# Route's shared network cut into 128 + 64 features, its list products one chunk later, the high digit's products on ScalarE

## Chip, cores, metric

The kernel runs on one NeuronCore of a Trainium2 chip. The metric is the device time of one launch in microseconds (us). Engines are named as in the profile: PE (TensorE; PEld is its weight load), DVE (VectorE), ACT (ScalarE), POOL (GpSimd), SP (SyncE, which here only issues DMAs).

## What is computed

The reference is a two-layer vision model on 8 images: patch embedding (1030 tokens of 192 features per image), retention, a mixture of experts, latent attention, a second mixture of experts. The change lies in the first mixture of experts. Its reference, cut to what matters:

```python
n = b * l                                   # 8 * 1030 tokens, d = 192
scores = sigmoid(x @ gate_weight.T)         # 16 experts
topk_score, topk_ids = top_k(scores.T, 1030)
xg = x[topk_ids]                            # each expert takes 1030 tokens
...
shared = silu(hidden_states @ Ws_g.T) * (hidden_states @ Ws_u.T) @ Ws_d.T   # 192 -> 384 -> 192
return y + shared
```

## The kernel before, in words

`phase_retention` ends with `x1T`, the normalised tokens with features on the partitions: two halves of 96 features (DP, DC = 96, 2). PE turns them (L385), ACT copies them out of PSUM (L499).

`phase_route` follows. It runs four instruction streams at once, bound only by semaphores; the order on each engine is that of the code.

- **Logits.** DVE copies the gate into a padded weight (L846), PE multiplies it with all tokens (L738), ACT applies the sigmoid.
- **The search**, LOOPS = 10 passes. Each pass finds three bits of the score threshold: DVE counts scores above a candidate (L862), PE sums the counts (`total`, L747), DVE keeps or drops the bit (L869 to L873). In between the pass does one chunk of 412 tokens of the shared network: gate and up in three slices f of 128 hidden features (`shared_up`, L715), silu on ACT (L800), the product on DVE (`shared_mult`, L825), down on PE (`shared_down`, L725), the sum with the residual on DVE (`shared_rows`, L834). SP loads and stores the rows.
- **A stretch on DVE** that turns the threshold into ranks, cut into a low digit (64 values) and a high digit (17 values), and PE turns them so that tokens lie on partitions.
- **The list stage**, NC = 10 chunks of 103 tokens, each with one more 412-token chunk of the shared network. DVE makes one-hot rows of the low digit (`hot_lo`, L928, four parts of 32 columns), of the high digit (`hit`, L933), and from `hit` two products: times the tile number (L937) and times the row number (L939), both into `hot_hi` (the trace calls it rt_wide). PE multiplies `hot_hi` with `hot_lo` (L785, 128 small products, "list products" below). `hot_lo` and `hot_hi` have two buffers each, `hit` one. POOL meanwhile issues 20 DMAs of scores (L705).

All of gate's and up's products are f32: the trace shows each as two records per product. In a chunk, slice f = 2 uses the PSUM banks of f = 0, so PE waits for the first `shared_mult`; `shared_down` waits for all three.

`phase_dispatch` and `phase_project`, late in the program, hold a shared network of the same size that is already cut into 128 + 64 (`shared_unit`, L2145 to L2151), with `pair_of` (L2132) on POOL. `phase_experts` has such a cut too. They are unchanged.

Of the kernel before, what the change touches and what calls it, by code (L numbers as in the profile page):

```python
# [16 lines left out]
B = 8  # L17
D = 192
# [220 lines left out]
def route_consts(ctx, nc):  # L239
    return buffers(ctx, nc, "rt", gate=(DP, DC, E0), same=(128, 128), before=(128, 128), consts32=(T, ROUTE_COLS), row=(T, 1),  # L240
                   wg=(DP, DC, FS0), wu=(DP, DC, FS0), wd=(128, FS0 // 128, D))


def load_route_consts(queue, inp, c, arrived):
    for dst, src in ((c["gate"][:], inp["gateT"].rearrange("(c p) e -> p c e", c=DC)),
                     (c["same"][:], inp["rt_same"]), (c["before"][:], inp["rt_before"]),
                     (c["consts32"][:], inp["rt_iota"]), (c["row"][:], inp["rt_row"]),
                     (c["wg"][:], inp["sh_gT"].rearrange("(c p) f -> p c f", c=DC)),
                     (c["wu"][:], inp["sh_uT"].rearrange("(c p) f -> p c f", c=DC)),
                     (c["wd"][:], inp["sh_dT"].rearrange("(c p) d -> p c d", c=FS0 // 128))):  # L250
        queue.dma_start(dst, src).then_inc(arrived, 16)


ROUTE_CONSTS = 16 * 8


def phase_retention(nc, psum, inp, h0, h1, xg, x1T, ident, ident_in, ret, consts_in, route, route_in):
# [5 lines left out]
    with ExitStack() as ctx:  # L263
# [105 lines left out]
        def _(pe):  # L369
# [9 lines left out]
            def turn_x1(c):  # L379

                for g in range(2):
                    pe.wait_ge(x_ready, c * 8 + (4 * g + 4))
                    for m in range(DC):
                        for b in range(HB):
                            last = pe.transpose(psum[0:DP, 2 * g + m, b * T:(b + 1) * T],  # L385
                                                x_out[:, g * HB + b, m * DP:(m + 1) * DP], ident[0:T, 0:T])
                        last.then_inc(xT_full, 1)
# [76 lines left out]
        def _(act):  # L464
# [30 lines left out]
            def x1_out(c):  # L495
                for g in range(2):
                    for m in range(DC):
                        act.wait_ge(xT_full, c * 4 + (2 * g + m + 1))
                        act.activation(x1T[:, m, g * HB:(g + 1) * HB, bass.ds(c * T, T)],  # L499
                                       bank(2 * g + m, DP, W4).rearrange("p (b t) -> p b t", b=HB),  # L500
                                       ACT.Identity).then_inc(xT_ready, 1)
# [102 lines left out]
def phase_route(nc, psum, inp, h1, xg, x1T, y, ids, ident, ident_in, consts, consts_in):  # L604
# [13 lines left out]
    with ExitStack() as ctx:  # L618
        sb, sem = names(ctx, nc)
        gate, same, before, consts32, row = (consts[n] for n in ("gate", "same", "before", "consts32", "row"))  # L620
        wg, wu, wd = (consts[n] for n in ("wg", "wu", "wd"))
        gpad = sb("rt_gpad", [DP, DC, B, 128])
        iota_lo = sb("rt_iota_lo", [T, LB], BF16)
        iota_hi = sb("rt_iota_hi", [T, HB2], BF16)
        tile0 = sb("rt_tile0", [T, 128], BF16)
# [37 lines left out]
        turned, turned_out = sem("rt_turned"), sem("rt_turned_out")  # L663
        hit_ready, hot_ready, hot_used = sem("rt_hit_ready"), sem("rt_hot_ready"), sem("rt_hot_used")
# [6 lines left out]
        h_loaded, y_stored = sem("sh_h_loaded"), sem("sh_y_stored")  # L671
# [24 lines left out]
        def _(pool):  # L696
            pool.memset(gpad[:], 0.0).then_inc(zeroed, 1)
            pool.memset(ones, 1.0).then_inc(zeroed, 1)
            pool.memset(zero[:], 0.0).then_inc(zeroed, 1)

            pool.wait_ge(turned_out, 9)
# [7 lines left out]
        def shared_up(pe, j, slices=range(FC)):  # L709

            for f in slices:
# [19 lines left out]
        def _(pe):  # L731
# [3 lines left out]
            for s, n in enumerate((W4, W4, SEQ - 2 * W4)):  # L735
                for b in range(B):
                    for k in range(DC):
# [38 lines left out]
            with pe.Fori(0, NC // 2) as i:  # L776
                for half in range(2):
                    c = i * 2 + half
                    shared_up(pe, c + LOOPS)
                    shared_down(pe, c + LOOPS)  # L780
                    pe.wait_ge(hot_ready, c + 1)
                    for b in range(B):
                        for e in range(E0):
                            q, g = e % 2, e // 2
                            last = pe.matmul(psum[LB * q:LB * q + 2 * HB2, 6, g * LB:(g + 1) * LB],  # L785
                                             hot_hi[:, half, b * E0 + e, :], hot_lo[:, half, b * E0 + e, :],
                                             start=False, stop=False, skip_group_check=True)
                    last.then_inc(hot_used, 1)
# [6 lines left out]
        def shared_silu(act, j):  # L795
            for f in range(FC):
# [6 lines left out]
        def _(act):  # L803
# [11 lines left out]
            with act.Fori(0, NC) as c:  # L815
                shared_silu(act, c + LOOPS)
# [22 lines left out]
        def _(dve):  # L839
# [3 lines left out]
            dve.wait_ge(zeroed, 3)  # L843
# [7 lines left out]
            dve.tensor_copy(tile0[:], consts32[:, LB + HB2:]).then_inc(consts_ready, 1)  # L851
# [69 lines left out]
            def list_chunk(c, half, first):  # L921
# [3 lines left out]
                if not first:  # L925
                    dve.wait_ge(hot_used, c - 1)
                for f in range(FC + 1):
                    dve.tensor_tensor(hot_lo[:, half, f * 32:(f + 1) * 32, :],  # L928
                                      lo_c[:, f * 32:(f + 1) * 32].unsqueeze(2).to_broadcast([T, 32, LB]),
                                      iota_lo[:].unsqueeze(1).to_broadcast([T, 32, LB]), ALU.is_equal)  # L930
                    if f < FC:
                        shared_mult(dve, c + LOOPS, (f,))
                dve.tensor_tensor(hit[:], hi_c.unsqueeze(2).to_broadcast([T, 128, HB2]),  # L933
                                  iota_hi[:].unsqueeze(1).to_broadcast([T, 128, HB2]), ALU.is_equal).then_inc(hit_ready, 1)
                dve.wait_ge(hit_ready, c * 2 + 1)

                dve.tensor_tensor(hot_hi[:, half, :, 0:HB2], hit[:], tile0[:].unsqueeze(2).to_broadcast([T, 128, HB2]),  # L937
                                  ALU.mult)
                dve.tensor_scalar(hot_hi[:, half, :, HB2:2 * HB2], hit[:], row[:, 0:1], None, ALU.mult) \  # L939
                    .then_inc(hot_ready, 1)  # L940
                dve.wait_ge(hot_ready, c + 1)
                dve.tensor_scalar(tile0[:], tile0[:], 1.0, None, ALU.add).then_inc(hit_ready, 1)
# [2385 lines left out]
def build(nc, inp, out):  # L3328
# [13 lines left out]
    with ExitStack() as ctx:  # L3342
# [7 lines left out]
        with ExitStack() as early:  # L3350
            route, ret = route_consts(early, nc), retention_consts(early, nc)
            phase_patches(nc, psum, inp, h0, ident, ident_in, ret, ret_in)
            x1T = early.enter_context(nc.sbuf_tensor("x1T", [DP, DC, B, SEQ], F32))[:]
# [121 lines left out]
```

## Time and profile before

| | |
|---|---|
| time, median of 3 runs | 4466.18 us (4458.52 to 4472.81) |
| the profiled execution | 4471.9 us, span 4470.2 us |
| busy in the span: PE, DVE, ACT, POOL | 88%, 56%, 32%, 28% |
| mean granted TensorE clock | 0.929 |
| `phase_route` in the span | about 455 to 871 us |

The span runs from the first to the last instruction of the profiled execution. A busy share is an average over phases with different limits. The granted clock is a share of TensorE's full clock; it has two levels, 1.2 and 2.4 GHz, so a mean of 0.88 over a stretch is a mix of both.

### The profile page before, as it was taken

To read this page: it belongs to the slowest core of one execution; us is meant where nothing else is said; L and a number is where in the kernel's file an instruction comes from. 1 tells how busy PE (TensorE), PEld (TensorE's weight loads), DVE (VectorE), ACT (ScalarE), POOL (GpSimd) and SP (SyncE) were. 2 spreads that over 40 slices of the span, in tenths; PEclk is the share of its full clock that TensorE was granted. 3 is DMA by queue.
4 is the path that set the end of the run, shared out by engine and by line. 5 is a ranking of instruction groups with operands and counts; after the bars stand their busy time and mean duration, and the time that the engine had idled before them with its cause. 6 is when DMAs were issued, how large, how long until landed. Compare 5 with 4: busy or idle time off the path is not lost. (4 is left out here: it accounts for less than half of the span.)

```text
span 4470.2 us, 74427 instructions
## 1 busy us (share of the span) xinstructions
PE 3951.7 (88%) x23896; PEld 2418.5 (54%) x23898; DVE 2508.2 (56%) x4595; ACT 1440.9 (32%) x2892; POOL 1271.0 (28%) x1439
## 2 busy tenths in 40 slices
PE   8899878699999998564999999999995998899996
PEld 8788555466666666332233333333333675577774
DVE  1576467632222222685887787778862547644442
ACT  0222110011111111233477777777772221111110
POOL 0221010134444443455000001000012112177775
PEclk9999998899999999776799999999996889999998
DMA  6221111223333331246232233322215431277776
GB/s 223 59 65 54 31 39 29 80 62 62 62 65 65 66 66 24 85 138 148 43 55 45 45 46 58 52 45 45 45 28 128 126 89 42 75 175 173 173 173 153
DMA packets 335969, 361.69 MB, mean 81 GB/s; under 512 B 50412, under 2 KB 297155, under 8 KB 334143
## 3 DMA queue, kind: packets, MB, share of 16 engines
q1 hardware_dynamic: 252207, 274.75, 25.2%
q0 software_dynamic: 61312, 63.66, 9.2%
q10 hardware_dynamic: 22288, 20.93, 1.5%
q8 instruction: 125, 2.05, 0.2%
q14 instruction: 37, 0.30, 0.0%
HBM read 247.51 MB, written 117.00 MB: 82 GB/s over the span
## 5 line engine op out<-in xcount | busy, mean ns | idle before, releaser
L2033 DVE TENSOR_REDUCE at_mx<-psum 128x1 f32<-128x998 f32 (+1 forms) x768 | 884.8, 1190 | 253.4 <-PE psum L1858 253.0
L1988 ACT ACTIVATE at_p<-psum 128x512 f32<-128x512 f32 (+3 forms) x1536 | 851.4, 588 | 299.2 <-PE psum L1932 269.1
L1932 PE MATMUL psum<-at_q,at_k 99*128 99x512 bf16 (+3 forms) x1536 | 521.5, 382 | 21.4 <-issue 16.4
L1858 PE MATMUL psum<-at_k,at_q 96*128 96x512 bf16 (+3 forms) x1536 | 475.6, 392 | 70.5 <-POOL at_identb L1815 33.1
L1918 PE MATMUL psum<-at_p,at_v 128*32 128x486 f32 (+3 forms) x3072 | 406.9, 602 | 1.0 <-ACT at_p L1988 0.7
L1932 PEld LDWEIGHTS psum<-at_q,at_k 99*128 99x128 bf16 (+1 forms) x1536 | 155.6, 102 | 426.2 <-ACT at_p L1988 272.0
L1224 DVE TENSOR_TENSOR ex_hT<-ex_silu,psum 128x384 f32<-128x384 f32 (+1 forms) x288 | 147.6, 512 | 415.8 <-ACT ex_silu L1193 270.6
L1193 ACT ACTIVATE ex_silu<-psum 128x384 f32<-128x384 f32 (+1 forms) x288 | 131.5, 456 | 772.9 <-PE psum L1137 642.8
L1830 POOL DMA_DIRECT2D o_rows<-at_o x96 | 48.5, 505 | 1145.5 <-DVE at_mx L2033 872.7
L1159 PE MATMUL psum<-ex_wd,ex_hT 128*128 128x192 f32 (+1 forms) x1728 | 291.5, 327 | 0.0
L1858 PEld LDWEIGHTS psum<-at_k,at_q 96*128 96x128 bf16 (+1 forms) x1536 | 152.4, 105 | 232.7 <-DVE at_mx L2033 64.0
L1159 PEld LDWEIGHTS psum<-ex_wd,ex_hT 128*128 128x128 f32 (+1 forms) x1728 | 264.2, 179 | 15.8 <-issue 3.6
L3136 POOL DMA_INDIRECT h_rows<-mx_ys,mx_to x144 | 229.2, 1592 | 59.7 <-issue 59.7
L3290 DVE TENSOR_TENSOR mx_hT<-mx_silu,psum 128x256 f32<-128x256 f32 x216 | 90.9, 421 | 270.1 <-ACT mx_silu L3247 177.8
L3247 ACT ACTIVATE mx_silu<-psum 128x256 f32<-128x256 f32 x216 | 82.8, 383 | 486.5 <-PE psum L3189 436.2
L1085 POOL DMA_INDIRECT y_rows<-ex_ys,ex_to x144 | 223.4, 1551 | 33.5 <-issue 33.5
L1132 PE MATMUL psum<-ex_xT,ex_wg 128*128 128x384 f32 (+1 forms) x576 | 230.9, 483 | 0.0
L1133 PE MATMUL psum<-ex_xT,ex_wu 128*128 128x384 f32 (+1 forms) x576 | 214.2, 454 | 0.0
L1138 PE MATMUL psum<-ex_xT,ex_wr 64*128 64x384 f32 (+1 forms) x576 | 205.3, 476 | 0.0
L1137 PE MATMUL psum<-ex_xT,ex_wr 64*128 64x384 f32 (+1 forms) x576 | 205.2, 476 | 0.0
L1050 POOL TENSOR_TENSOR ex_pad<-ident 128x1 f32<-128x1 f32 x127 | 41.5, 327 | 436.3 <-DVE ex_ys L1237 429.2
L1237 DVE TENSOR_TENSOR ex_ys<-psum,ex_score 128x384 f32<-128x384 f32 (+1 forms) x80 | 41.2, 515 | 205.6 <-PE psum L1159 205.6
(378 smaller groups left out, 7067.5 us busy)
## 6 DMA issues: line engine op xcount, KB each, us to landing
mx_wd<-in_e_dT SPq DMA_DIRECT2D x72, 288.0 KB, 4.1
qk_parts<-hd_parts SPq DMA_DIRECT2D x32, 579.4 KB, 3.8
at_k<-qk_parts SPq DMA_DIRECT2D x144, 128.8 KB, 5.4
at_q<-qk_parts SPq DMA_DIRECT2D x144, 124.8 KB, 4.6
tok_p<-in_x SPq DMA_DIRECT2D x12, 1176.0 KB
mx_wg<-in_e_gT SPq DMA_DIRECT2D x72, 192.0 KB, 2.5
mx_wu<-in_e_uT SPq DMA_DIRECT2D x72, 192.0 KB, 2.8
v_rows<-hd_v_out SPq DMA_DIRECT2D x8, 1536.0 KB
```

What stands on the lines that cost most here:

```text
L1085: pool.indirect_dma_start(y, bass.IndirectOffsetOnAxis(ap=to[0:n, half, t:t + 1], axis=0), ys[0:n, half, t, :], None, compute_op=ALU.add). ...
L1132: g = pe.matmul(gate, wg[:, half, cols], xT[:, 0, toks], start=first, stop=not first)
L1133: u = pe.matmul(lift, wu[:, half, cols], xT[:, 0, toks], start=first, stop=not first)
L1137: g = pe.matmul(gate, wr[0:64, half, cols], xT[0:64, 1, toks], start=first, stop=not first)
L1138: u = pe.matmul(lift, wr[64:128, half, cols], xT[64:128, 1, toks], start=first, stop=not first)
L1159: mm = pe.matmul(psum[0:n, 4 + p % 2, (t % 2) * D:(t % 2 + 1) * D], hT[:, f, 128 * t:128 * t + n], wd[:, half, f, :], start=(f == 0), stop ...
L1858: mm = pe.matmul(psum[0:ctx_rows[t], 3 + 2 * ((PRO + n) % 2) + k, 0:w], Q[v][0:R6, j * 1024 + 128 * t:j * 1024 + 128 * t + ctx_rows[t]], K ...
L1918: mm = pe.matmul(psum[32 * j:32 * j + HV, 7, 0:w], V[u][0:n, t, j * HV:(j + 1) * HV], P[0:n, c % 2, j, 0:w], start=(t == 0), stop=(t == CT ...
L1932: pe.matmul(psum[0:n, i % RING, 0:w], K[u][:, j, 128 * t:128 * t + n], Q[u][:, j * 1024 + at:j * 1024 + at + w], start=True, stop=True).th ...
L1988: act.activation(P[0:n, c % 2, j, 0:w], psum[0:n, i % RING, 0:w], ACT.Exp).then_inc(exp_ready, 1)
L2033: dve.tensor_reduce(mx[0:ctx_rows[t], j * CT + t:j * CT + t + 1], pair(n)[0:ctx_rows[t], 0:CTX], AX_X, ALU.max).then_inc(s_free, 1)
L3136: pool.indirect_dma_start(y, bass.IndirectOffsetOnAxis(ap=to[:, r, t:t + 1], axis=0), ys[:, r, t, :], None, compute_op=ALU.add).then_inc(a ...
```

## The change

Four edits, all in what leads to and makes up `phase_route`:

1. `x1T` has 128 partitions: part 0 holds features 0 to 127; part 1 holds features 64 to 191, of which only the upper half (128 to 191) is used. The gate weight is padded with zeros to match.
2. `shared_up` does a slice as `most` (gate and up, 128 features each) and `remainder` (gate's 64 features on array rows 0 to 63, up's 64 on rows 64 to 127). The order is most, remainder for f = 0 and 2, remainder, most for f = 1. POOL copies the chunk's last 64 features into both halves of `xr` (`pair_up`) once the chunk before has left `shared_up`.
3. `list_rows(c)` stands between `shared_up` and `shared_down` of the next chunk.
4. ACT makes the two products of the high digit (`high_digits`): one over all 2176 columns between silu 0 and 1, eight of 272 columns (one for each image, with the tile number of that image as the scale) between silu 1 and 2. DVE makes `hit` first in the chunk, copies the eight tile numbers, and no longer does L937, L939 and L942.

```diff
-                   wg=(DP, DC, FS0), wu=(DP, DC, FS0), wd=(128, FS0 // 128, D))
+                   wg=(128, FS0), wu=(128, FS0), wr=(128, FS0), wd=(128, FS0 // 128, D))
...
+            def pair_up(j):
+                pool.wait_ge(u_full, j * FC)
+                for half in range(2):
+                    pool.tensor_tensor(carried[0:16, half:half + 1], zero32[0:16], zero32[0:16], ALU.add)
+                    pool.tensor_copy(xr[64 * half:64 * half + 64], x_flat[64:128, 1, bass.ds(j * W4, W4)]).then_inc(xr_ready, 1)
+                    pool.wait_ge(xr_ready, j * 2 + (half + 1))
+            with pool.Fori(0, LOOPS + 1) as j:
+                pair_up(j)
             pool.wait_ge(turned_out, 9)
...
+            with pool.Fori(LOOPS + 1, 2 * LOOPS) as j:
+                pair_up(j)
...
             for f in slices:
-                pe.wait_ge(hT_ready, j * FC + max(f - 1, 0)) if f else pe.wait_ge(hT_ready, j * FC)
-                for w, n, full in ((wg, 0, g_full), (wu, 1, u_full)):
-                    for k in range(DC):
-                        last = pe.matmul(psum[:, 2 * (f % 2) + n, 0:W4], w[:, k, f * 128:(f + 1) * 128],
-                                         x_flat[:, k, bass.ds(j * W4, W4)], start=(k == 0), stop=(k == 1))
-                    last.then_inc(full, 1)
+                if f == 0:
+                    pe.wait_ge(xr_ready, j * 2 + 2)
+                pe.wait_ge(hT_ready, j * FC + max(f - 1, 0))
+                def most(first):
+                    g = pe.matmul(gate, wg[:, cols], toks, start=first, stop=not first)
+                    u = pe.matmul(lift, wu[:, cols], toks, start=first, stop=not first)
+                def remainder(first):
+                    g = pe.matmul(gate, wr[0:64, cols], xr[0:64], start=first, stop=not first)
+                    u = pe.matmul(lift, wr[64:128, cols], xr[64:128], start=first, stop=not first)
+                if f % 2 == 0:
+                    most(True)
+                    g, u = remainder(False)
+                else:
+                    remainder(True)
+                    g, u = most(False)
+                g.then_inc(g_full, 1)
+                u.then_inc(u_full, 1)
...
+            def high_digits(c, half):
+                act.wait_ge(hit_ready, c + 1)
+                act.activation(hot_hi[:, half, :, HB2:2 * HB2], hit[:], ACT.Copy, scale=row[:, 0:1])
+                shared_silu(act, c + LOOPS, (1,))
+                for b in range(B):
+                    last = act.activation(hot_hi[:, half, b * E0:(b + 1) * E0, 0:HB2], hit[:, b * E0:(b + 1) * E0, :],
+                                          ACT.Copy, scale=tile_now[:, half, b:b + 1])
+                last.then_inc(hot_ready, 1)
...
             for b in range(B):
-                last = dve.tensor_copy(gpad[:, :, b, b * E0:(b + 1) * E0], gate[:])
+                dve.tensor_copy(gpad[:, 0, b, b * E0:(b + 1) * E0], gate[:, 0, :])
+                last = dve.tensor_copy(gpad[64:128, 1, b, b * E0:(b + 1) * E0], gate[64:128, 1, :])
```

DVE at the end of a chunk of the list stage, before (rt_wide is `hot_hi`, sh_hT the result of `shared_mult`, sh_y_out that of `shared_rows`):

```order
L928 TENSOR_TENSOR rt_hot_lo<-rt_loT,rt_iota_lo 103x2048
L825 TENSOR_TENSOR sh_hT<-sh_silu,psum 128x412
L928 TENSOR_TENSOR rt_hot_lo<-rt_loT,rt_iota_lo 103x2048
L933 TENSOR_TENSOR rt_hit<-rt_hiT,rt_iota_hi 103x2176
L937 TENSOR_TENSOR rt_wide<-rt_hit,rt_tile 103x128x17
L939 TENSOR_SCALAR rt_wide<-rt_hit,rt_row 103x128x17
L942 TENSOR_SCALAR rt_tile<-rt_tile 103x128
L834 TENSOR_TENSOR sh_y_out<-psum,sh_h_in 103x384 x2
```

DVE now, from the last third of one chunk into the next:

```order
L999 TENSOR_TENSOR rt_hot_lo<-rt_loT,rt_iota_lo 103x2048
L888 TENSOR_TENSOR sh_hT<-sh_silu,psum 128x412
L999 TENSOR_TENSOR rt_hot_lo<-rt_loT,rt_iota_lo 103x2048
L897 TENSOR_TENSOR sh_y_out<-psum,sh_h_in 103x384 x2
L995 COPY rt_tile_now<-rt_tiles 103x8
L996 TENSOR_TENSOR rt_hit<-rt_hiT,rt_iota_hi 103x2176
L999 TENSOR_TENSOR rt_hot_lo<-rt_loT,rt_iota_lo 103x2048
L888 TENSOR_TENSOR sh_hT<-sh_silu,psum 128x412
```

L937, L939 and L942 are gone from behind `hit`; `hit` (L996) and a copy of eight columns (L995) stand ahead of the first `hot_lo`, and so ahead of the chunk's first `shared_mult`.

PE in the list stage before, from up's last slice into the next chunk:

```order
L715 MATMUL psum<-x1T,rt_wu 128x412 x2
L721 REGISTER_ALU
L722 REGISTER_ALU
L725 MATMUL psum<-rt_wd,sh_hT 103x192 x12
L781 REGISTER_ALU
L785 MATMUL psum<-rt_hot_lo,rt_wide 34x64 x128
L712 ISA
L715 ISA
L715 MATMUL psum<-x1T,rt_wg 128x412
```

PE now, from the last slice of chunk c + 1 to the start of chunk c + 2 (L739 and L740 are the 128 features, L744 and L745 the 64; L820 is the list products of chunk c):

```order
L739 MATMUL psum<-x1T,rt_wg 128x412
L740 MATMUL psum<-x1T,rt_wu 128x412
L744 MATMUL psum<-sh_xr,rt_wr 128x412
L745 MATMUL psum<-sh_xr,rt_wr 128x412
L815 REGISTER_ALU
L820 MATMUL psum<-rt_hot_lo,rt_wide 34x64 x128
L759 REGISTER_ALU
L763 MATMUL psum<-rt_wd,sh_hT 103x192 x12
L733 ISA
L734 REGISTER_ALU
L739 ISA
L739 MATMUL psum<-x1T,rt_wg 128x412
```

The list products stood behind down (L725) of their own chunk; they now stand ahead of down (L763) of the chunk after it.

ACT in one chunk of the list stage now, where before it had three silu (L800) alone:

```order
L848 ACTIVATE sh_silu<-psum 128x412
L866 REGISTER_ALU
L867 ACTIVATE rt_wide<-rt_hit,rt_row 103x128x17
L845 REGISTER_ALU
L848 ACTIVATE sh_silu<-psum 128x412
L870 ACTIVATE rt_wide<-rt_hit,rt_tile_now 103x16x17 x8
L845 REGISTER_ALU
L848 ACTIVATE sh_silu<-psum 128x412
```

Nine instructions over `hit` stand between the silu of slice 0 and that of slice 2.

## Rows read from the trace of the kernel before

**Rows 1.** Windows (from:to, length; busy us; granted clock, DMA share, GB/s): search, list stage.

```profile
490.00:631.00 141.00, 131.39 (x540) 89.30 (x540) 84.63 (x261) 28.19 (x40) 0.00 (x0) 1.00 0.15 41
...
653.00:867.00 214.00, 169.72 (x1760) 120.38 (x1761) 172.21 (x130) 15.61 (x31) 13.68 (x20) 0.88 0.12 31
```

**Rows 2.** Timeline, one pass of the search: start us, us, engine line op, [idle before].

```profile
560.22 1.55 PE L715 MATMUL psum<-x1T,rt_wg 96*128 x4
...
560.42 0.56 DVE L834 TENSOR_TENSOR sh_y_out<-psum,sh_h_in 103x384 f32<-103x384 f32 x1 [0.96 <-PE psum L725]
...
563.29 0.58 DVE L825 TENSOR_TENSOR sh_hT<-sh_silu,psum 128x412 f32<-128x412 f32 x1 [0.91 <-PE psum L715]
...
565.98 0.30 PE L747 MATMUL psum<-rt_count,rt_same 128*128 128x1 f32 x2
...
569.29 0.58 DVE L825 TENSOR_TENSOR sh_hT<-sh_silu,psum 128x412 f32<-128x412 f32 x1 [0.45 <-PE psum L715]
...
570.00 2.19 PE L725 MATMUL psum<-rt_wd,sh_hT 128*103 128x192 f32 x12 [0.85 <-DVE sh_hT L825]
...
574.19 1.55 PE L715 MATMUL psum<-x1T,rt_wg 96*128 x4
```

**Rows 3.** Timeline, one chunk of the list stage, from its list products to the next.

```profile
760.76 3.51 PE L785 MATMUL psum<-rt_hot_lo,rt_wide 103*34 103x64 bf16 x128 [3.51 <-DVE rt_wide L939]
...
764.19 1.65 PE L715 MATMUL psum<-x1T,rt_wg 96*128 x4
...
767.07 1.55 PE L715 MATMUL psum<-x1T,rt_wg 96*128 x4
...
767.34 0.58 DVE L825 TENSOR_TENSOR sh_hT<-sh_silu,psum 128x412 f32<-128x412 f32 x1 [3.11 <-PE psum L715]
...
767.84 2.28 DVE L928 TENSOR_TENSOR rt_hot_lo<-rt_loT,rt_iota_lo 103x2048 bf16<-103x2048 bf16 x1
...
768.45 1.55 PE L715 MATMUL psum<-x1T,rt_wu 96*128 x4
...
773.59 4.14 PE L725 MATMUL psum<-rt_wd,sh_hT 128*103 128x192 f32 x24 [0.83 <-DVE sh_hT L825]
...
775.57 2.42 DVE L933 TENSOR_TENSOR rt_hit<-rt_hiT,rt_iota_hi 103x2176 bf16<-103x2176 bf16 x1
...
781.24 3.51 PE L785 MATMUL psum<-rt_hot_lo,rt_wide 103*34 103x64 bf16 x128 [3.51 <-DVE rt_wide L939]
```

**Rows 4.** Timeline, PE behind the first list products of the stage.

```profile
673.18 3.12 PE L715 MATMUL psum<-x1T,rt_wg 96*128 x4
```

**Rows 5.** Timeline in `phase_dispatch`: 64-feature products of 412 columns, then 128-feature ones.

```profile
3802.80 0.61 PE L2150 MATMUL psum<-di_xr,di_wr 64*128 64x412 f32 x1
...
3802.81 0.61 PE L2151 MATMUL psum<-di_xr,di_wr 64*128 64x412 f32 x1
...
3804.39 0.96 PE L2145 MATMUL psum<-x3T,di_wg 128*128 x2
```

**Rows 6.** Instructions of ACT by shape in the whole span: busy us, mean ns, idle before.

```profile
L800 ACT ACTIVATE sh_silu<-psum 128x412 f32<-128x412 f32 x60 | 30.8, 513 | 276.6 <-PE psum L715 276.6
...
L2842 ACT ACTIVATE di_silu<-psum 128x206 f32<-128x206 f32 x15 | 5.1, 343 | 29.7 <-PE psum L2150 21.7 <-PE psum L2145 8.0
```

**Rows 7.** POOL's copies of 64 features in `phase_dispatch` (ns min/median/max), and DVE beside one.

```profile
L2132 POOL COPY di_xr<-x3T_rest x10: 1038/1044/3556, 3691.6 to 3822.3; 64x1030 f32<-64x1030 f32 x10
...
3786.34 3.23 DVE L3005 TENSOR_TENSOR di_hot_hi<-di_hit,di_codes 128x2592 bf16<-128x2592 bf16 x1
...
3790.42 2.85 DVE L3009 TENSOR_TENSOR di_hot_hi<-di_hit,di_codes 128x2592 bf16<-128x2592 bf16 x1
```

**Rows 8.** Timeline of POOL at the start of the list stage.

```profile
653.51 13.68 POOL L705 DMA_DIRECT2D x_rows<-rt_scT  x20 [194.84 <-ACT rt_scT L813]
```

**Rows 9.** What L428 (retention) waits for: us, times; then the gate's copies.

```profile
  ACT x1T L499: 7.8, 16
...
458.71 0.77 DVE L846 COPY rt_gpad<-rt_gate 96x32 f32<-96x32 f32 x8 [3.00 <-POOL rt_zero L699]
```

More of the change, by code:

```diff
@@ L736, in _ @@
                 for b in range(B):
-                    for k in range(DC):
+                    for k in range(2):
                         last = pe.matmul(psum[:, s, 0:n], gpad[:, k, b, :], x1T[:, k, b, s * W4:s * W4 + n],
@@ L775, in _, with list_rows @@
             pe.wait_ge(turned_out, 9)
-            with pe.Fori(0, NC // 2) as i:
+            def list_rows(c, half):
+                pe.wait_ge(hot_ready, c + 1)
+                pe.wait_ge(lo_ready, c + 1)
+                for b in range(B):
+                    for e in range(E0):
+                        q, g = e % 2, e // 2
+                        last = pe.matmul(psum[LB * q:LB * q + 2 * HB2, 6, g * LB:(g + 1) * LB],
+                                         hot_hi[:, half, b * E0 + e, :], hot_lo[:, half, b * E0 + e, :],
+                                         start=False, stop=False, skip_group_check=True)
+                last.then_inc(hot_used, 1)
+            shared_up(pe, LOOPS)
+            shared_down(pe, LOOPS)
+            with pe.Fori(0, NC // 2 - 1) as i:
                 for half in range(2):
                     c = i * 2 + half
[L779 to L788, printed above, removed]
+                    shared_up(pe, c + LOOPS + 1)
+                    list_rows(c, half)
+                    shared_down(pe, c + LOOPS + 1)
+            shared_up(pe, NC - 1 + LOOPS)
+            list_rows(NC - 2, 0)
+            shared_down(pe, NC - 1 + LOOPS)
+            list_rows(NC - 1, 1)
             pe.matmul(LISTS, zero[:, 0:128], zero[:], start=False, stop=True, skip_group_check=True).then_inc(ids_full, 1)
@@ L793, in _, with shared_silu @@
             last.then_inc(idT_full, 1)
-        def shared_silu(act, j):
-            for f in range(FC):
+        def shared_silu(act, j, slices=range(FC)):
+            for f in slices:
                 act.wait_ge(g_full, j * FC + (f + 1))
@@ L926, in list_chunk @@
                     dve.wait_ge(hot_used, c - 1)
-                for f in range(FC + 1):
-                    dve.tensor_tensor(hot_lo[:, half, f * 32:(f + 1) * 32, :],
-                                      lo_c[:, f * 32:(f + 1) * 32].unsqueeze(2).to_broadcast([T, 32, LB]),
-                                      iota_lo[:].unsqueeze(1).to_broadcast([T, 32, LB]), ALU.is_equal)
+                if not (first and half == 0):
+                    dve.wait_ge(hot_ready, c)
+                dve.tensor_copy(tile_now[:, half, :], tiles[:, bass.ds(c, 1), :].rearrange("p c b -> p (c b)"))
+                dve.tensor_tensor(hit[:], hi_c.unsqueeze(2).to_broadcast([T, 128, HB2]),
+                                  iota_hi[:].unsqueeze(1).to_broadcast([T, 128, HB2]), ALU.is_equal).then_inc(hit_ready, 1)
+                for f in range(FC + 1):
+                    low = dve.tensor_tensor(hot_lo[:, half, f * 32:(f + 1) * 32, :],
+                                            lo_c[:, f * 32:(f + 1) * 32].unsqueeze(2).to_broadcast([T, 32, LB]),
+                                            iota_lo[:].unsqueeze(1).to_broadcast([T, 32, LB]), ALU.is_equal)
+                    if f == FC:
+                        low.then_inc(lo_ready, 1)
                     if f < FC:
                         shared_mult(dve, c + LOOPS, (f,))
[L933 to L942, printed above, removed]
                 shared_rows(dve, c + LOOPS)
```

53 lines of the change are left out of this document (36 added, 17 removed).

## The prediction, made before the changed kernel was run

> **What bounds the kernel now.** The change touches one phase, so I read that phase and not the shares of the whole span. First the windows by stage: in the search PE is busy 131 of 141 us at a granted clock of 1.00; in the list stage DVE is busy 172 and PE 170 of 214 us, at a mean clock of 0.88 [rows 1]. Neither is full there, so the two take turns, and the timeline must say how.
>
> In the search one pass lasts 574.19 - 560.22 = 13.97 us [rows 2]. PE runs through except at three places that DVE releases: `total` at 565.98, which waits for the count, and down at 570.00, which stands idle 0.85 us for the last `shared_mult` (569.29). PE and DVE are both in the chain.
>
> In the list stage one chunk lasts 781.24 - 760.76 = 20.48 us [rows 3]. The list products start when DVE has made `hot_hi`, after PE has stood idle 3.51 us. Then PE does up, and DVE stands idle 3.11 us for it, until its first `shared_mult` at 767.34. So the loop is: list products 3.43 us (760.76 to 764.19), up to the first mult 3.15, three mults and three `hot_lo` 8.23 (to 775.57), `hit` and its two products 5.67. The whole stage takes from 653.5 [rows 8] to 781.24 + 4 x 20.48 + 3.43 = 866.6, that is 213.1 us, against 10 x 20.48 = 204.8. The other 8.3 us are chunks in which PE ran at the lower clock: behind the first list products four records take 3.12 us [rows 4] where they take 1.65 [rows 3].
>
> **Prices.** One f32 product of 412 columns: two in 768.45 - 767.07 = 1.38, so 0.69 us [rows 3]. The 64-feature products are in this trace, in another phase. Gate's and up's start 0.01 us apart and end together, so both cost one. Four record pairs, two slices, take 3804.39 - 3802.80 = 1.59 us, 0.21 more than 1.38, and the first wide records behind them take 0.96 against 0.85 without a switch (1.55 for four less 0.70 for two): so every change between 128 rows and 64 rows costs about 0.21 us, half inside and half outside the block [rows 3, 5]. In the Trainium skill, "TensorEngine Tiling (Array Packing)", Key Properties, changing the tiling mode drains the array; it gives no time for it, and by its speedup of 2 alone a slice would fall from 4 products to 3. The rows agree that there is a drain. A slice thus costs 1.38 + 0.21 + 0.69 = 2.28 us where it cost 2.76; slices 0 and 1 together 4.56, since their narrow parts touch.
>
> ACT: 513 ns for 412 columns and 343 for 206 is 0.825 ns a column and 0.17 us fixed [rows 6]. The product over 2176 columns is then 1.97 us, each of the eight of 272 columns 0.40. These rows read PSUM or f32; here it is bf16 in SBUF with a stride, which no row shows. Lower bound as priced; upper, DVE's 2.42 us for `hit`'s 2176 columns [rows 3], a factor of 1.2. A chunk of ACT is 1.97 + 3.2 + 3 x 0.51 = 6.7 us.
>
> POOL: 1.04 us for 1030 columns, up to 3.56 beside DVE's products of two SBUF operands, which themselves go from 2.85 to 3.23 [rows 7]. For 412 columns: 0.42 to 1.42, and two of them with two tiny operations 1.3 to 3.4 us.
>
> **The search.** I let the pass start at 0 (560.22). Up's slice 0 now ends at 2.28, gate and up together. Silu starts 0.2 later and takes 0.51, so the first mult is at 3.05; before it was at 3.07, because it waited for up and gate was early [rows 2]. Nothing behind it moves: the second `total` still waits for the count, at 5.76. Slice 1, with three switches more at the totals, ends about 5.2, in time. Slice 2 starts at 5.92 and ends at 8.20; its silu is now all behind PE, and the last mult comes at 8.20 + 0.2 + 0.51 + 0.04 = 8.95 against 9.07. Down follows it by 0.71 as before. Gain 0.12 us a pass, **-1.2 us** in ten (bounds -4, if the mult came with slice 2's wide part, and +5, if each of six switches a pass cost 0.1 more). So 2 x 0.69 us less of PE work in each slice goes into an exposed silu and the wait for the count. POOL's pair starts at about 8.5 and has until 13.9: hidden even at 3.4.
>
> **The list stage.** Time 0 is the end of down on PE. DVE's second `shared_rows` starts 0.2 later and it is free at 0.7 [rows 2]. Then the tile numbers 0.1, `hit` 2.45, the first `hot_lo` 2.25: the first mult is at 5.5. PE has done slices 0 and 1 at 4.56 and waits for it, until 5.5 + 0.7 = 6.2. That is the new wait, 1.65 us, and what stands behind it is slice 2, the list products and down. Slice 2 with the switch out of it ends at 8.7, list products 3.43 to 12.1, down 574.19 - 570.00 - 0.15 = 4.04 to **16.2** [rows 2, 3]. The other chains are inside: mults every 8.23 / 3 = 2.74, so the last at 11.0 and down could go at 11.7; ACT has `hit` at 3.25, the wide product to 5.25, silu 1 to 5.8, the eight to 9.0, silu 2 to 9.5, needed at 11.0; POOL's pair runs from 8.9 to at most 12.3, needed at 16.2. DVE's own work is 14.1 us, PE's 14.5.
>
> A chunk falls from 20.48 to 16.2. The first has no list products: mults at 658.2, 661.0 and 663.7, down from 664.4 to 668.4. POOL is then busy with its DMAs until 667.2 [rows 8] and has xr at 668.5 to 670.6; slices 0 and 1 have 1.65 us to spare, so this costs nothing up to 670.1. End: 668.4 + 9 x 16.2 + 3.43 = 817.6 against 866.6, **-49.0 us**. Of this 8.3 are low-clock chunks that I leave out of the new stage; their condition was 3.5 us of idle PE before small products, and now 1.65 is left in a chunk, but once 3.2 (661.2 to 664.4). I put back **+2**, bounds 0 and +8.3. For DVE beside POOL's copies, 0.38 us a copy of 1030 columns [rows 7], so 0.3 a chunk against 0.4 of slack: **+1**, bounds 0 and +3.
>
> **The rest.** Sixteen gate copies for eight (0.77 us) before the logits [rows 9]: **+0.8**. Logits: same columns, 0. The 160 turns load 128 columns for 96; PE stands idle 7.8 us behind ACT's copies of them [rows 9], which covers 49 ns each, and the last chunk is open: 0, bounds 0 and +3. Three more DMAs on SP before the first chunk of retention: 0, other loads run there for many us.
>
> Sum: -49.0 - 1.2 + 2 + 1 + 0.8 = -46.4. Against the profiled execution's 4471.9 that is 4425.5; it ran 5.7 above the median of 4466.18, from which I get **4420 us**. The bounds add to -52 and -27; with 4 us for the spread of the median, 4410 to 4443.
>
> **Rivals.**
> - *The clock falls in every chunk.* The wait of 1.65 us and the sparse list products might do what 3.5 us did in some chunks. Price as in the chunks of before: 8.3 us over three, 2.8 each, nine times 25: about 4443. For it: a mean clock of 0.88 in the stage. Against: later chunks ran 20.48 each with the longer idle and no fall, and the search has idle places too at 1.00 [rows 1]. 12 in 100.
> - *Contention.* POOL's copies and DVE's two-operand products slow each other [rows 7]. If DVE lost 0.38 us in each of two copies and PE waited for all of it, 9 x 0.76 = 7 us, and in the search some tenths a pass: about 4430. It lies in the range. 10 in 100. The Trainium skill, "GPSIMD Engine Reference", says that contention arises with DVE instructions with two SBUF inputs, and `hot_lo` is one; the trace agrees, with 3.56 against 1.04 us.
> - *ACT becomes the bound: slower than before.* Place: silu 2 stands behind the eight products, and down behind silu 2. From `hit` at 3.25 ACT has 7.7 us until it is needed at 11.0, plus 0.4 of slack, for 6.2 us of work: it bites above a factor of 1.3. It decides when a chunk costs 5.4 us more than 16.2, that is at 6.2 + 1.9 + 5.4 = 13.5 us, or 2.2 times the price of the rows. At 2.5 times: 15.5, 7.4 a chunk, +67 - 46: 4487. Against it: `hit` itself, on DVE, reads and writes such columns at one a cycle. 4 in 100.
> - *The order does nothing*: if DVE after `shared_rows` were the whole chain, the gain is only the work taken from DVE, 5.67 - 2.45 = 3.2 us a chunk, 29 in nine: 4435. In the range, 8 in 100.
> - Something outside my sums, either way, 6 in 100, of which 3 no change.
>
> My forecast (4405 to 4430) has 60. All but four cases are faster, so the range reaches from 4405 to 4445 and leaves out a gain over 61 us, ACT over 1.4 times, and the cases outside. A measurement of this kernel can tell about 0.3%, 13 us, from no change. Faster 0.92, within 0.04, slower 0.04.
>
> **What would show it.** In the profile after: list chunks 16.2 us apart, PE idle about 1.7 us before slice 2 with DVE's mult as the releaser, a search pass of 13.8 to 13.9 us, ACT's copies 2.0 and 0.4 us, POOL's under 1.5, the clock above 0.95 in the list stage. I am wrong if the pass of the search gets longer by over 0.5 us, if PE waits for `sh_xr`, or if silu 2 is the releaser of the last mult.

## The result, and the profile after

The changed kernel takes 4419.2 us, the median of 4 runs (4415.23 to 4424.8), beside 4469.5 for the kernel before in the same comparison (4 runs, 4458.52 to 4475.47). The ratio is 0.9882, with an interval of 0.9867 to 0.9896. The profiled execution took 4417.4 us with a span of 4415.7, so 54.5 us less between the two spans and 50.3 between the medians.

Where those 54.5 us lie follows from two marks, POOL's first score DMA (653.51 before, [rows 8]; 656.7 after) and the copy of the finished lists (867.0 before, 813.4 after). Up to the list stage the new kernel loses 3.2 us, in the list stage it gains 213.5 - 156.7 = 56.8, and behind it it gains another 0.9. Of the 3.2 us, 2.8 are the gate's copies (below); the whole phase also begins 0.7 us later. Neither 0.7 nor 0.9 us says anything of the change: in the profiled executions of this document the phase begins between 453.4 and 458.3 us, and the part behind the list stage, which no kernel here changes, takes 3591.9 to 3608.5 us.

The windows of the changed kernel: the search, the list stage, and one set of list products (columns as in [rows 1]).

```profile
490.00:628.00 138.00, 120.77 (x532) 74.06 (x530) 82.47 (x253) 28.46 (x41) 13.11 (x38) 1.00 0.16 41
...
651.00:815.00 164.00, 139.38 (x1789) 94.61 (x1790) 140.07 (x112) 71.53 (x129) 58.35 (x56) 0.98 0.17 40
...
742.50:744.40 1.90, 1.90 (x130) 1.90 (x128) 1.90 (x2) 1.04 (x3) 1.72 (x1) 1.00 0.00 0
```

The same for two sets of list products of the kernel before, that of [rows 3] first:

```profile
760.80:764.10 3.30, 3.30 (x128) 3.30 (x128) 3.23 (x4) 0.00 (x0) 0.00 (x0) 0.51 0.32 84
...
740.40:743.70 3.30, 3.30 (x128) 3.26 (x126) 3.23 (x4) 0.00 (x0) 0.00 (x0) 0.52 0.33 88
```

These short windows are the main finding. Before, the 128 list products of the chunk in [rows 3] ran at a granted clock of 0.51, the lower level of 1.2 GHz, behind 3.51 us in which PE stood idle, and those of the chunk ahead of it at 0.52. After, PE comes to them straight from up, the clock is 1.00 (2.4 GHz), and they take 2.04 us instead of 3.51. The mean of 0.88 in [rows 1] had spread this over the stage.

The timeline of the changed kernel, one chunk of the list stage (start us, us, engine line op, [idle before]), answers to [rows 3]:

```profile
749.39 0.85 PE L739 MATMUL psum<-x1T,rt_wg 128*128 x2
...
750.29 2.42 DVE L996 TENSOR_TENSOR rt_hit<-rt_hiT,rt_iota_hi 103x2176 bf16<-103x2176 bf16 x1
...
752.75 2.15 ACT L867 ACTIVATE rt_wide<-rt_hit,rt_row 103x2176 bf16<-103x2176 bf16 x1 [0.37 <-DVE rt_hit L996]
...
755.18 3.44 ACT L870 ACTIVATE rt_wide<-rt_hit,rt_tile_now 103x272 bf16<-103x272 bf16 x8
...
755.46 0.96 PE L739 MATMUL psum<-x1T,rt_wg 128*128 x2 [1.36 <-DVE sh_hT L888]
...
757.94 2.04 PE L820 MATMUL psum<-rt_hot_lo,rt_wide 103*34 103x64 bf16 x128
...
758.13 2.23 POOL L712 TENSOR_TENSOR sh_carried<-sh_zero 16x1 f32<-16x1 f32 x1 [9.88 <-PE psum L745]
...
760.40 0.53 POOL L713 COPY sh_xr<-x1T 64x412 f32 x1
...
760.85 4.15 PE L763 MATMUL psum<-rt_wd,sh_hT 128*103 128x192 f32 x24 [0.87 <-DVE sh_hT L888]
...
763.16 0.53 POOL L713 COPY sh_xr<-x1T 64x412 f32 x1
...
764.84 0.85 PE L739 MATMUL psum<-x1T,rt_wg 128*128 x2
```

This chunk lasts 764.84 - 749.39 = 15.45 us; the mean of the last nine is 15.35. PE waits twice in it, 1.36 us in front of slice 2 and 0.87 in front of down, and DVE's mult ends both waits. The waits of the whole stage say the same (waiter, releaser, us, times, longest):

```profile
PE psum L739 <- DVE sh_hT L888: 11.8, 10, 1.4
...
PE psum L763 <- DVE sh_hT L888: 10.7, 10, 2.8
```

The longest of 2.8 us is in the first chunk, which has no list products. Down behind it takes 5.83 us, where in the other chunks it takes 4.15 (timeline, PE):

```profile
667.12 5.83 PE L763 MATMUL psum<-rt_wd,sh_hT 128*103 128x192 f32 x24 [2.85 <-DVE sh_hT L888]
```

The timeline of one pass of the search, as in [rows 2]:

```profile
563.53 0.85 PE L739 MATMUL psum<-x1T,rt_wg 128*128 x2
...
566.61 0.58 DVE L888 TENSOR_TENSOR sh_hT<-sh_silu,psum 128x412 f32<-128x412 f32 x1 [0.88 <-ACT sh_silu L848]
...
569.22 0.38 PE L785 MATMUL psum<-rt_count,rt_same 128*128 128x1 f32 x2 [0.46 <-DVE rt_junk L928]
...
573.25 2.20 PE L763 MATMUL psum<-rt_wd,sh_hT 128*103 128x192 f32 x12 [1.27 <-DVE sh_hT L888]
...
577.44 0.85 PE L739 MATMUL psum<-x1T,rt_wg 128*128 x2
```

The pass is 13.91 us beside 13.97. The first mult comes 3.08 us into it (3.07 before), now released by silu and no longer by PE. What PE does less has become idle: 1.27 us before down instead of 0.85, and 0.46 for the count. The start of the phase, the gate's copies (timeline; before: [rows 9]):

```profile
456.24 1.81 POOL L702 MEMSET rt_gpad<- 128x2048 f32 x1 [32.44 <-POOLq L62]
...
460.04 0.45 DVE L910 COPY rt_gpad<-rt_gate 64x16 f32<-64x16 f32 x1
...
463.16 29.92 PE L776 MATMUL psum<-x1T,rt_gpad 128*128 128x412 f32 x96 [10.17 <-DVE rt_gpad L910]
```

From the memset to the first logit product 6.9 us pass. In the kernel before they were 4.1 (455.5 to 459.6).

### The profile page after: what moved, and what is told of

It reads as the page before. It is cut to its first block and busy times, and to the rows that moved or that the text cites. A ratio compares the mean times of both kernels' runs of the same rounds, so it can differ in the third digit from the quotient of the medians.

```text
span 4415.7 us, 74709 instructions
## 1 busy us (share of the span) xinstructions
PE 3907.1 (88%) x23896; PEld 2372.0 (54%) x23898; DVE 2477.4 (56%) x4583; ACT 1494.8 (34%) x2982; POOL 1333.3 (30%) x1520
```

## The experiments

All ratios are to the kernel before. "List stage" runs from POOL's first score DMA to the copy of the lists, in the profiled execution. Times of one kernel lie up to 23 us apart between executions, so a stage is read from a profile and only the total from the ratio. A gain given in us "by the ratio" is the ratio's share of the median of the kernel before.

**Each part alone.** The recorded expectations weigh three theories. Theory 1: the clock and DVE's queue set the list stage, PE's amount of work does not. Theory 2: the list products take 3.4 us at any clock, as the prediction priced them. Theory 3: the three parts share the gain about equally. Three kernels take one part each.

The core of `act_alone`, in which the order on PE stays as before:

```diff
-                dve.tensor_tensor(hot_hi[:, half, :, 0:HB2], hit[:], tile0[:].unsqueeze(2).to_broadcast([T, 128, HB2]),
...
-                dve.tensor_scalar(hot_hi[:, half, :, HB2:2 * HB2], hit[:], row[:, 0:1], None, ALU.mult) \
...
+                act.activation(hot_hi[:, half, :, HB2:2 * HB2], hit[:], ACT.Copy, scale=row[:, 0:1])
...
+                    last = act.activation(hot_hi[:, half, b * E0:(b + 1) * E0, 0:HB2], hit[:, b * E0:(b + 1) * E0, :],
```

> The kernel before with one of the three parts: ACT makes the high digit's products, hit stands first on DVE. List products stay behind down of their own chunk, the shared network keeps 96 + 96 features. Theory 1 (the clock and DVE's queue set the list stage, PE's work does not): the products are ready when down ends, PE does not stand idle before the list products, so they run at the full clock in 1.9 us for 3.5; a chunk is then DVE's chain of 5.5 us to the first mult, two steps of 2.74, 0.7 and down 4.04, 15.7 us, and the kernel is 50 to 55 us faster than before. Theory 2 (list products cost 3.4 us at any clock, as I priced them before the result): a chunk is 16.7 us and the gain 37 to 42 us. Theory 3 (the three parts share the gain about equally): 17 us faster.

Measured: 4414.89 us, ratio 0.9878 (0.9857 to 0.9898); list stage 158.7. By the ratio this is 55 us, as theory 1 expected (50 to 55), and as much as the whole change gives. Two rows of PE in its timeline show why:

```profile
743.17 4.14 PE L726 MATMUL psum<-rt_wd,sh_hT 128*103 128x192 f32 x24 [0.86 <-DVE sh_hT L845]
...
747.24 2.04 PE L783 MATMUL psum<-rt_hot_lo,rt_wide 103*34 103x64 bf16 x128
```

The list products follow down with no wait and take 2.04 us: ACT had finished the high digits at 738.61 + 3.43 = 742.04, before down began. The old place of the list products costs nothing once what they need is early.

In `later_alone` DVE makes all products of the high digit as before, and PE's loop is written out of step:

```diff
-                    shared_up(pe, c + LOOPS)
-                    shared_down(pe, c + LOOPS)
-                    pe.wait_ge(hot_ready, c + 1)
...
+                    shared_up(pe, c + LOOPS + 1)
+                    list_rows(c, half)
+                    shared_down(pe, c + LOOPS + 1)
```

> The kernel before with one of the three parts: the list products of a chunk stand between up and down of the next one. Theory 1: DVE keeps all its work and is then the bound, 17.7 us a chunk of 20.5 to 23.6, and the kernel is about 33 us faster; the list products run in 1.9 us since PE comes from up. Theory 2 gives the same time within 2 us but list products of 3.4 us. Theory 3: 17 us faster.

Measured: 4433.52 us, 0.9928 (0.9906 to 0.9949); list stage 174.9. Nine of its ten sets of list products take 2.04 us and wait for nothing; only the last set of the stage, which comes behind down, follows 2.4 us of idle and takes 3.07. But DVE still makes all products of the high digit, works almost without a pause, and so its work sets the chunk: two chunks together take 34.4 us, 17.2 each. The 32 us by the ratio are what theories 1 and 2 both gave; the 2.04 us speak against theory 2.

`split_alone` has the 128 + 64 features alone: the wider turns, the gate's sixteen copies, POOL's pair, and the pass in which gate's and up's 64 features share the array:

```diff
+                    g = pe.matmul(gate, wr[0:64, cols], xr[0:64], start=first, stop=not first)
+                    u = pe.matmul(lift, wr[64:128, cols], xr[64:128], start=first, stop=not first)
```

> The kernel before with one of the three parts: 128 + 64 features, gate's and up's 64 in one pass, the padded gate in sixteen copies. Theory 1: PE's work falls by about 1.2 us a chunk but the first silu now waits for gate and up together, so a chunk of the list stage stays at 20.3 to 20.5 us, a pass of the search at 13.9, and the start of the phase is 3 us longer: between 2 us faster and 4 us slower than before. Theory 3: 17 us faster.

Measured: 4466.39 us, 0.9992 (0.9981 to 1.0003), no measurable change, and not the 17 us of theory 3; list stage 204.8, search pass 13.90. The profiled execution is the fastest of ten, 10.7 us under their median, so the 8.7 us by which its list stage is shorter than before are not shown to be a gain. The clock fell there in other places: behind 3.85 us of idle the list products took 2.53 to 3.30 us, behind 2.2 us of idle 3.44 to 3.57 in three chunks and 2.04 in one, and behind 2.06 us of idle down took 5.83 us instead of 4.15 in four of ten chunks.

**Filling the idle before the list products.** These two kernels are the kernel before with more work for PE, products of zeros into a PSUM bank that nothing reads, put where PE waits for `hot_hi`. If the idle and the clock are what made the list products slow, a kernel that does more gets faster; if not, it cannot.

```diff
                     shared_down(pe, c + LOOPS)
+                    for n in range(14):
+                        pe.matmul(psum[:, 7, :], zero[:, 0:128], zero[:], start=True, stop=True, skip_group_check=True)
                     pe.wait_ge(hot_ready, c + 1)
```

> The kernel before with 14 bf16 products of 512 columns of zeros into a free PSUM bank, placed where PE waits for the high digit's products in each chunk of the list stage; work is added, none is taken away. Theory 1: the idle 3.5 us is what drops TensorE's clock; with the fill of about 3.0 us the granted clock stays at 1.00, the list products take 1.9 us for 3.5, up is never at half speed, a chunk is 18.9 us and the kernel is 20 to 25 us faster although it does more. Theory 2 (the small products cost 3.4 us for themselves): no change, within 3 us.

Measured: 4451.9 us, 0.9961 (0.9947 to 0.9975); list stage 191.5, 22.0 us less than before. By the ratio the kernel gains 17 us (11 to 24); the profiled execution was the fastest of seven. Timeline, PE, one chunk:

```profile
739.91 4.14 PE L725 MATMUL psum<-rt_wd,sh_hT 128*103 128x192 f32 x24 [0.82 <-DVE sh_hT L827]
...
743.89 3.19 PE L782 MATMUL psum<-rt_zero 128*128 128x512 bf16 x14
...
747.56 2.04 PE L787 MATMUL psum<-rt_hot_lo,rt_wide 103*34 103x64 bf16 x128 [0.49 <-DVE rt_wide L941]
...
758.93 4.14 PE L725 MATMUL psum<-rt_wd,sh_hT 128*103 128x192 f32 x24 [0.83 <-DVE sh_hT L827]
```

The list products start as late as before, 7.65 us behind the start of down, since DVE's chain is the same, but they run at full clock, and the chunk is 19.02 us for 20.48.

`fill_small` has 208 products of the size of the list products in the same place:

```diff
+                    for n in range(208):
+                        q = n % 2
+                        pe.matmul(psum[LB * q:LB * q + 2 * HB2, 7, 0:LB], zero[0:T, 0:2 * HB2], zero[0:T, 0:LB], start=True, stop=True, skip_group_check=True)
```

> The kernel before with 208 small bf16 products of 34 x 64 of zeros, alternating between PSUM partitions 0 and 64 as the list products do, where PE waits for the high digit's products. Theory 1: two column halves work side by side, so they run at 15 ns each while the clock is full, 3.1 us in all. If small products keep the clock, the list products take 1.9 us and the gain is that of the wide fill, 20 to 25 us. If they do not, they themselves drift to 27 ns, run past the wait, and the kernel is from no change to 15 us slower. Theory 2: each costs 27 ns from the first one on, 5.6 us, 20 us slower than before.

Measured: 4454.79 us, 0.9974 (0.9962 to 0.9986); list stage 193.7. The filler, in the shape of the list products, takes 3.21 us for 208, 15 ns each, and the list products behind it again 2.04 in eight of ten chunks; in the first two they are interrupted once, for 1.07 and 0.67 us, by no wait that the profile shows. The granted clock of the list stage is 1.00 in both kernels, so products as sparse as these hold the clock as well as wide ones did. By the ratio the gain is 12 us (6 to 17), less than the 20 to 25 that I expected, with the profiled execution the fastest of ten.

**Each part undone in the changed kernel.** The edits are the diffs above in reverse, applied to the changed kernel.

> The changed kernel with DVE making the high digit's products as before; list products later and the split stay. Theory 1: DVE's own work of 17.7 us bounds the chunk; 28 to 33 us faster than the kernel before, that is some 20 us slower than the changed one. Theory 3 (three equal parts): 34 us faster than before.

Measured: 4433.15 us, 0.9932 (0.9912 to 0.9952); list stage 180.3. By the ratio 30 us, within theory 1's 28 to 33, but theory 3's 34 is not told apart from it by this run. The stage is 5.4 us longer than that of `later_alone`, which has no 64-feature pass, and it has a wait that `later_alone` cannot have, PE for the copies of POOL (us, times, longest):

```profile
PE psum L738 <- POOL sh_xr L712: 10.4, 9, 5.0
```

In the list stage of the changed kernel PE never waits for these copies.

> The changed kernel with the list products back behind down of their own chunk; the split and ACT's products stay. Theory 1: with ACT's products the list products never wait, wherever they stand; PE's order costs nothing since the chunk is DVE's chain of 15.5 to 15.7 us: within 3 us of the changed kernel, 47 to 52 us faster than before. Theory 2 (a wait for hot_hi comes back): 35 us faster. Theory 3: 34 us faster.

Measured: 4440.76 us, 0.9944 (0.9925 to 0.9963); list stage 173.9. My expectation missed: this kernel is `act_alone` with the 64-feature pass, and loses 15.2 us of list stage against it. Its timeline, one chunk:

```profile
752.16 0.49 ACT L842 ACTIVATE sh_silu<-psum 128x412 f32<-128x412 f32 x1
...
752.69 0.58 DVE L882 TENSOR_TENSOR sh_hT<-sh_silu,psum 128x412 f32<-128x412 f32 x1 [0.56 <-ACT sh_silu L842]
...
753.32 5.83 PE L763 MATMUL psum<-rt_wd,sh_hT 128*103 128x192 f32 x24 [2.79 <-DVE sh_hT L882]
...
759.08 2.04 PE L820 MATMUL psum<-rt_hot_lo,rt_wide 103*34 103x64 bf16 x128
```

The 64-feature pass ends gate's accumulation together with up's, so silu 0, ACT's wide product behind it and in the end silu 2 come later, and the last mult waits 0.56 us for it. PE now stands idle 2.79 us in front of down, where `act_alone` had 0.86: of the 1.93 us more, 0.56 is that wait, and the rest is near 1.4, three slices that PE does 0.48 us faster each. In seven of ten chunks down then took 5.50 to 7.06 us instead of 4.15, 12.3 us in all. `act_alone` has one such down too, the first of its stage, with 5.69 us, so 10.7 of the 15.2 us are slower downs, and about 0.5 us in each chunk is the later last mult.

> The changed kernel with 96 + 96 features and gate and up in four products a slice; the padded gate in eight copies, POOL copies nothing. Theory 1: the chunk stays at 15.5 to 15.7 us because DVE's chain sets it, the search pass goes from 13.91 to 13.97, and the start gets back 3 us: 50 to 56 us faster than before, so up to 4 us faster than the changed kernel. Theory 3: 34 us faster than before.

Measured: 4411.59 us, 0.9891 (0.9863 to 0.9919); list stage 155.6. Without the 128 + 64 features the kernel is no slower.

**Improving it.** `gate_in_eight` clears the unused gate rows and copies all 128 rows in eight copies again.

```diff
+            pool.memset(gate[0:64, 1, :], 0.0).then_inc(zeroed, 1)
...
-                dve.tensor_copy(gpad[:, 0, b, b * E0:(b + 1) * E0], gate[:, 0, :])
-                last = dve.tensor_copy(gpad[64:128, 1, b, b * E0:(b + 1) * E0], gate[64:128, 1, :])
+                last = dve.tensor_copy(gpad[:, :, b, b * E0:(b + 1) * E0], gate[:])
```

> The changed kernel with the padded gate filled in eight DVE copies again: the unused half of the gate's second part is zeroed by POOL ahead of the phase's other memsets, so one copy fills both parts. Theory: sixteen copies cost 2.8 us more than eight did before, on the path to the logits, because each small copy takes its full 0.17 to 0.2 us and does not overlap; back to 1.0 us more than before at most. Expected 1.5 to 2.8 us faster than the changed kernel in the time from gpad's memset to the first logit product (6.9 us there, 4.1 before), which the medians cannot resolve.

Measured: 4415.93 us, 0.9876 (0.9859 to 0.9894); from the memset to the logits 4.5 us (455.23 to 459.73) for 6.9.

`dve_order` begins a chunk's DVE work with one `hot_lo` and mult 0, so that PE gets its mult earlier. ACT does silu 1 before its wide product and silu 2 before its eight.

```diff
+                low(0)
+                shared_mult(dve, c + LOOPS, (0,))
                 dve.tensor_tensor(hit[:], hi_c.unsqueeze(2).to_broadcast([T, 128, HB2]),
                                   iota_hi[:].unsqueeze(1).to_broadcast([T, 128, HB2]), ALU.is_equal).then_inc(hit_ready, 1)
...
+                shared_mult(dve, c + LOOPS, (1,))
+                low(1)
+                shared_mult(dve, c + LOOPS, (2,))
+                low(2)
+                low(3).then_inc(lo_ready, 1)
```

> The changed kernel with another order in a chunk of the list stage: DVE does hot_lo 0, mult 0, hit, mult 1, hot_lo 1, mult 2, hot_lo 2 and 3; ACT does silu 0, silu 1, the wide product, silu 2, the eight products. Same work. Theory 1 (DVE's queue in front of mult 0 and mult 2 is what PE waits for): the waits of 1.2 to 1.4 and 0.87 us go, DVE's own work of 14.2 us becomes the chunk, 15.45 now, and the kernel is about 11 us faster than the changed one, 61 to 65 us than the one before. Rival (PE's 14.5 us or POOL's copies, which end 1.1 us ahead of PE's need, become the bound): a chunk stays at or above 15 us and the gain is under 4 us.

Measured: 4413.97 us, 0.987 (0.9854 to 0.9886); list stage 152.1, 4.6 us less than the changed kernel, less than half of the 11 us that I expected, though a chunk takes 14.3 us and not the 15 of the rival. The timeline shows the new wait:

```profile
758.55 2.11 POOL L712 TENSOR_TENSOR sh_carried<-sh_zero 16x1 f32<-16x1 f32 x1
...
760.71 2.50 POOL L713 COPY sh_xr<-x1T 64x412 f32 x1
...
763.45 0.95 PE L739 MATMUL psum<-x1T,rt_wg 128*128 x2 [0.89 <-POOL sh_xr L713]
```

PE no longer waits for mult 0 but for POOL's second copy, which beside DVE's `hot_lo` took 2.50 us.

`both_edits` is the changed kernel with these two edits.

> The two edits above together. Theory 1: 12 to 14 us faster than the changed kernel, 62 to 67 us faster than the one before.

Measured: 4408.08 us, 0.9862 (0.9846 to 0.9877); list stage 152.2.

`order_without_split` is `dve_order` without the 128 + 64 features.

> The new order of DVE and ACT with list products later, but 96 + 96 features as before the change. Theory 1: PE has 8.3 + 1.9 + 4.0 = 14.2 us of work in a chunk, DVE 14.2 as well, so a chunk is 14.2 to 14.8 us; the start is 2.8 us shorter than in the changed kernel; 64 to 70 us faster than the kernel before, so not slower than both edits with the split. Rival (the split is needed once DVE no longer waits): a chunk of 15.5 us or more, under 55 us faster.

Measured: 4407.33 us, 0.9856 (0.9842 to 0.9869); list stage 145.9. There is no copy of POOL's to wait for, and PE goes from list products to down to the next up without a gap, so that a chunk takes 14.35 us, PE's own work (timeline, PE):

```profile
750.37 2.04 PE L783 MATMUL psum<-rt_hot_lo,rt_wide 103*34 103x64 bf16 x128
...
752.34 4.15 PE L726 MATMUL psum<-rt_wd,sh_hT 128*103 128x192 f32 x24
...
756.33 1.55 PE L716 MATMUL psum<-x1T,rt_wg 96*128 x4
```

This version and `both_edits` are the fastest, and the intervals don't tell them apart. Against the changed kernel they overlap too, if little: 9 and 12 us by the ratios, not settled by these runs. The list stages of their profiled executions are 4.5 and 10.8 us shorter than that of the changed kernel.

## Why the prediction was right, and where its terms were not

The total was right (4420 forecast, 4419.2 measured), and its mechanism held: the list stage falls by a fourth, DVE's mult is the new releaser, the search hardly moves. That the two totals agree within 1 us is luck. Between the two profiled executions the forecast was 46.4 us and 54.5 were measured: the list stage gained 10.8 us more than forecast, the part ahead of it lost 3.6 more, and 0.9 came from behind it. Between the medians there are 50.3 us, and the forecast was taken off a median of 4466.18 (3 runs) where that of the comparison is 4469.5 (4 runs).

- **The list products** are the mis-sized term. I priced them at 3.43 us, their time in [rows 3], and took only the 8.3 us of slow chunks as clock. In fact that row itself was at 0.51; at full clock they take 2.04. So a chunk is 15.35 us in the mean and not 16.2 (7.6 us in nine), and the last set of list products is 1.4 shorter. The 3 us that I had put back for clock and contention are not seen beyond that, the first chunk is 1.2 longer than I had it, and the stage gained 56.8 instead of 46. The ten sets of list products took 34.4 us before and 20.4 after, 14.0 less; with the 8.3 the clock had cost about 22 us of the stage. `fill_wide` gives back 22.0 in its profiled execution (11 to 24 by the ratio) while it changes nothing in DVE's chain. That the clock made the list products slow is thereby shown; that it is 22 of the 56.8 is arithmetic on one execution of each. The other 35 us or so go to the shorter chain, by the same arithmetic.
- **Slice 2's wait** was forecast at 1.65 us, measured 1.2 to 1.36 (0.48 in the first chunk). In front of down PE waits 0.87 for mult 2; I had the list products end after that mult, at 12.1 against 11.7, and with them at 2.04 it is the other way round. DVE's queue is the chunk's chain.
- **Gate copies**, forecast +0.8, cost +2.8. I scaled [rows 9]'s 0.77 us for eight, a time for copies that overlap. The sixteen smaller ones came one behind the other at 0.17 to 0.19 us each, and two, each beside a copy of POOL's, stretched to 0.45. `gate_in_eight` gives back 2.4.
- **The search**: 13.91 against a forecast of 13.85; -0.6 us in ten passes instead of -1.2. **One pass for both 64s** and the 0.21 us of a switch held: slices with the pass start with 0.85 and, behind a switch, 0.96, as in [rows 5].
- **ACT** took 2.14 us for the wide product and 0.43 for each of the eight, where I had 1.97 and 0.40; a factor of 1.1, well under the 1.3 from which it bites. DVE waited for none of its silus in the list stage of the changed kernel. In `without_later` it did, by the order of its queue and not by its price.
- **POOL's pair** takes 5.6 us (758.13 to 763.16 + 0.53 = 763.69), past my upper bound of 3.4. I scaled the copies and gave the tiny operations nothing. It still ends 1.15 us before PE needs it, so it cost nothing here; it held PE up in `without_act` and became the bound in `dve_order`.
- **The retention turns** cost nothing: a run of sixteen takes 2.98 us beside 2.96.
- **The rivals.** The clock in every chunk: wrong for this kernel, but I had argued against it from a misread row. I wrote that the later chunks of the kernel before showed "no fall", and their list products ran at 0.51 and 0.52. Only the first chunk of the changed kernel shows it, where the 3.2 us that I had named is 2.85 of idle and down loses 1.68 us, near the 2 that I had put back. Contention: there, but hidden. ACT as the bound: no. The order does nothing: half true, since `act_alone` gives the whole gain with the old order on PE, but that gain is not the 29 us of work taken from DVE.
- **The range.** The bounds of the single terms add to about -52 and -29, not -27; with that the range ends 2 us lower.
- **The parts.** The prediction priced the change as a whole and gave no part its share. ACT's part alone gives 0.9878, later products alone 0.9928, the pass 0.9992; the first two are two ways to the same end, list products that need not wait, and do not add up. The 64-feature pass takes 1.4 us of PE work out of three slices, in a chunk in which PE waits anyway.

What stays open: why the clock falls sooner behind one idle stretch than behind another, since in `split_alone` list products behind 3.85 us of idle lost less than most of those behind 2.2 us; and by how much low-clock chunks vary from one execution to the next. `without_later` ran between 4428.49 and 4448.77 us, with the profiled one the shortest, and a varying number of slow downs would do that, but only one execution of each kernel has a trace.

## What to carry to other kernels

A duration taken from a trace carries the clock it ran at: read the granted clock of exactly those instructions before it becomes a term, above all behind an idle stretch. Work that sits behind a wait of PE can cost the wait and then the slow products; here giving PE its input earlier gave back both, and filler in the idle gave back the second. And less work on an engine that waits can lengthen its idle and so slow what follows, as the 64-feature pass did in `without_later`: test the parts of a change apart, because the one that looks best by its count of instructions may be worth nothing.

## What the runs showed of the hardware

- Small products of 64 columns that alternate between PSUM partitions 0 and 64 took 15 to 16 ns each at full clock (208 in 3.21 us, 128 in 2.04). In the list stage of `fill_small` the granted clock was 1.00 with 208 of them as filler; in the kernel before, behind 3.51 us of idle the 128 list products took 3.51 us at 0.51.
- Where PE idled 2.8 us in front of down, the 24 products took 5.83 us and up to 7.06 instead of 4.15, but not in each chunk (seven of ten, `without_later`). Behind 2.06 us of idle it was four of ten (`split_alone`, 5.83).
- A POOL operation on one column of 16 partitions takes 0.18 us in the search and over 2 us beside DVE's `hot_lo`, an operation with two SBUF operands, longer than the copy of 412 columns behind it. The groups of the changed kernel (busy us, mean ns):

```profile
L712 POOL TENSOR_TENSOR sh_carried<-sh_zero 16x1 f32<-16x1 f32 x40 | 39.2, 979 | 231.8 <-PE psum L745 229.8 <-POOL sh_zero L705 0.2
...
L713 POOL COPY sh_xr<-x1T 64x412 f32 x40 | 21.2, 530 | 1.7
```

The mean of 979 ns mixes the two. The Trainium skill, "GPSIMD Engine Reference", Specifications, says that contention arises with DVE instructions of two SBUF inputs; the trace agrees, with 2.23 us for the operation on 16x1 beside `hot_lo`.
